# Two-layer routed FFN around causal linear attention: the third norm's moments in two halves, and the state's copy and mask moved to ScalarE and GpSimd

## The reference

```
def _layernorm(x, axis=-1, eps=1e-05):
    return (x - mean) / sqrt(var + eps)

def _L0_ffn_ref(x, Wg, W1, b1, W2, b2):            # 8 experts, 128 -> 512 -> 128
    top_w, top_i = top_k(x @ Wg, 2); top_w = softmax(top_w)
    for i in range(8):
        out_i = gelu(x @ W1[i] + b1[i]) @ W2[i] + b2[i]
        results = results + w_per_expert[..., i:i+1] * out_i

def _L0_attn_ref(x, ...):                          # 16 heads of 8
    q, k = phi(x @ Wq.T + bq), phi(x @ Wk.T + bk)  # phi = elu + 1
    v = x @ Wv.T + bv
    kv_prefix = cumsum(k outer v, axis=tokens);  k_prefix = cumsum(k)
    out = (q . kv_prefix) / (q . k_prefix + 1e-6)
    return merge_heads(out) @ Wo.T + bo

x = x + 0.5 * ffn(layernorm(x))
x = x + attn(layernorm(x))
x = x + 0.5 * ffn(layernorm(x))
```

## Time and profile before

| | |
|---|---|
| median of 3 runs | 378.76 us (378.44 to 379.9) |
| profiled execution, its own time | 379.24 us |
| its span, first to last instruction | 377.5 us |
| busy: PE / DVE / POOL / ACT | 81% / 61% / 60% / 33% |
| attention loop (164.4 to 238.4 us), busy: PE / DVE / POOL / ACT | 65.66 / 68.57 / 42.84 / 31.62 us |
| ScalarE's waits for stores of the ring | 6.7 us in 6 |

### The profile page before, as it was taken

How to read it: one execution, slowest core, us unless ns; L and a number is a source line. 1 busy time by engine, 2 the same in 40 slices (tenths; PEclk the granted TensorE clock), 3 DMA queues, 4 the chain that set the end, 5 groups by cost and what they waited for, 6 DMA issues and landing times.

```text
span 377.5 us, 7941 instructions
## 1 busy us (share of the span) xinstructions
PE 305.7 (81%) x1941; PEld 241.6 (64%) x1942; DVE 229.1 (61%) x620; ACT 122.8 (33%) x344; POOL 226.0 (60%) x266
## 2 busy tenths in 40 slices
PE   2984799898989975689999997557989888989950
PEld 1932499787878861256767675423989777878820
DVE  6899344334333337979989898995344433433456
ACT  2206243322323340234444553253333232332300
POOL 5037577777777770264584845265577777777720
PEclk9997699999999997589999999665899999999995
DMA  7530466555545527100000000013565555545347
GB/s 214 166 102 2 113 191 183 151 159 163 150 144 166 142 71 202 29 0 0 3 0 10 14 16 16 21 43 106 125 193 161 160 160 142 168 137 156 112 130 224
DMA packets 34918, 41.90 MB, mean 111 GB/s; under 512 B 4753, under 2 KB 21265, under 8 KB 34898
## 3 DMA queue, kind: packets, MB, share of 16 engines
q1 hardware_dynamic: 29906, 31.44, 30.0%
q0 software_dynamic: 4992, 10.23, 8.9%
HBM read 33.39 MB, written 8.26 MB: 110 GB/s over the span
## 4 chain that ended last, share of the span: by engine, by line
POOL 33%; PE 26%; DVE 13%; DMA 12%; issue 12%; ACT 2%; SPq 0%; POOLq 0%; DVEq 0%; ACTq 0%
POOL y_rows L405 15%; POOL xg L398 13%; PE banks L987 5%; PE banks L1093 5%; DMA xg<-xn_rows,src_row 4%; PE banks L996 3%; DMA y_rows<-y_tile,dst_row 3%; DMA xn_rows<-xn_ring 2%; POOL kv L427 2%; DMA y_back<-y_rows 2%; DVE x L789 2%; PE banks L1072 2%; PE banks L917 2%; DVE x L794 2%; DVE beats L651 1%
## 5 line engine op out<-in xcount | busy, mean ns | idle before, releaser
L398 POOL DMA_INDIRECT xg<-xn_rows,src_row x78 | 75.5, 968 | 33.3 <-issue 23.4
L405 POOL DMA_INDIRECT y_rows<-y_tile,dst_row x78 | 76.8, 985 | 24.6 <-issue 21.4
L987 PE MATMUL banks<-xgT,w1b 128*128 128x128 f32 x624 | 88.3, 286 | 0.8 <-ACT xgT L507 0.8
L996 PE MATMUL banks<-w,h_act 128*128 x624 | 87.7, 284 | 0.4 <-issue 0.2
L746 DVE TENSOR_TENSOR h_pre<-banks,w1b 128x512 f32<-128x512 f32 x78 | 53.9, 691 | 55.6 <-PE banks L987 51.5
L987 PEld LDWEIGHTS banks<-xgT,w1b 128*128 128x128 f32 x624 | 78.3, 197 | 2.7 <-issue 1.2
L996 PEld LDWEIGHTS banks<-w,h_act 128*128 128x128 f32 x624 | 75.5, 191 | 5.8 <-issue 2.6
L756 DVE COPY y_tile<-banks 128x128 f32<-128x128 f32 x78 | 22.7, 292 | 65.5 <-DMA y_rows<-y_tile,dst_row 57.9
L507 ACT COPY xgT<-banks 128x128 f32<-128x128 f32 x78 | 20.7, 265 | 126.1 <-PE banks L1006 126.1
L514 ACT ACTIVATE h_act<-h_pre 128x512 f32<-128x512 f32 x78 | 49.3, 632 | 4.7 <-DVE h_pre L746 4.7
L427 POOL TENSOR_TENSOR kv<-qk,vx 128x1024 f32<-128x1024 f32 x16 | 31.5, 1970 | 29.8 <-DVE qk L775 29.8
(11 more groups left out here) (185 smaller groups left out, 395.3 us busy)
## 6 DMA issues: line engine op xcount, KB each, us to landing
w1b<-in_W1b SPq DMA_DIRECT2D x78, 258.0 KB
y_back<-y_rows SPq DMA_DIRECT2D x16, 256.0 KB, 4.9
xg<-xn_rows,src_row POOLq DMA_INDIRECT x78
y_rows<-y_tile,dst_row POOLq DMA_INDIRECT x78
x<-in_L_attn_x SPq DMA_DIRECT2D x4, 256.0 KB, 3.6
xn_rows<-xn SPq DMA_DIRECT2D x4, 256.0 KB, 3.0
xn_rows<-xn_ring SPq DMA_DIRECT2D x16, 64.0 KB, 1.5
out<-x SPq DMA_DIRECT2D x4, 256.0 KB, 2.9
```

Of the source, the lines that this page charges most:

```text
L398: g.indirect_dma_start(out=xg[:, n % RING, :], out_offset=None, in_=xn_rows[f][:, :], in_offset=bass.IndirectOffsetOnAxis(ap=src_row[:, n: ...
L405: g.indirect_dma_start(out=y_rows[f][:, :], out_offset=bass.IndirectOffsetOnAxis(ap=dst_row[:, i:i + 1], axis=0), in_=y_tile[:, i % RING, ...
L987: last = mm(h_bank(q)[:, c * P:(c + 1) * P], w1b[:, q, c * P:(c + 1) * P], xgT[:, q, :], start=True, stop=True)
L996: last = mm(y_bank(r), h_act[:, r, c * P:(c + 1) * P], w2[:, bass.ds(col + c * P, P)], start=(c == 0), stop=(c == FC - 1))
```

## The change

The third norm's work on GpSimd is cut in two: the seven instructions come behind `outer` of tiles 7, 11 and 15, and 1/root and shift in a function of their own, `ln3_roots`, behind `outer` of tiles 9 and 13 and behind the loop. VectorE's L859 is gone: ScalarE copies the state out of PSUM to a new tile `state_raw`, behind `pre` and in front of the next `norm`, and GpSimd multiplies that by the mask (`own_heads`), for tile i-1 at the end of its work for tile i. The state matmul of the last tile is left out. `norm_3` writes to `xn`, which the first FFN no longer needs, and no ring is left; its lag is 11 tiles for 8, and SyncE stores four tiles at a time.

```
                 else:
-                    rows = xn_rows[1].rearrange("(t p) d -> t p d", p=P)
-                    for t in range(NT):
-                        sp.wait_ge(xn_ready, NT + t + 1)
-                        sp.wait_ge(xn_stored, 16 * (NC + t))
-                        sp.dma_start(rows[t], xn_ring[:, t % 2, :]).then_inc(xn_stored, 16)
+                    rows = xn_rows[1].rearrange("(t p) d -> p t d", p=P)
+                    for c in range(NC):
+                        sp.wait_ge(xn_ready, NT + CH * (c + 1))
+                        sp.dma_start(rows[:, c * CH:(c + 1) * CH, :], xn[:, c * CH:(c + 1) * CH, :]).then_inc(xn_stored, 16)
...
-                pool.wait_ge(xn_stored, 16 * (NC + NT * f))
+                pool.wait_ge(xn_stored, 16 * NC * (f + 1))
...
                 g.tensor_tensor(var_3[:, :], var_3[:, :], apart_3[:, :], ALU.add).then_inc(ln3_step, 1)
+
+            def ln3_roots(b):
+
+                t = b * CH
                 pool.wait_ge(ln3_step, b * 7 + 7)
                 g.tensor_tensor(rstd_3[:, t:t + CH], var_3[:, :], minus_half[:, 0:CH], ALU.pow).then_inc(ln3_root, 1)
...
+            def own_heads(i):
+
+                pool.wait_ge(raw_sb, i + 1)
+                pool.wait_ge(inter_ps, i + 1)
+                g.tensor_tensor(state[:, :], state_raw[:, :], head_mask[:, :, :].rearrange("p e h -> p (e h)"),
+                                ALU.mult).then_inc(state_sb, 1)
 
             for i in range(NT):
                 outer(i)
...
-                if i >= CH + 2 and i % CH == 2:
+                if i > CH and i % CH == 3:
                     ln3_moments(i // CH - 1)
+                if i > 2 * CH and i % CH == 1:
+                    ln3_roots(i // CH - 2)
+                if 0 < i:
+                    own_heads(i - 1)
+            ln3_roots(NC - 2)
             ln3_moments(NC - 1)
+            ln3_roots(NC - 1)
             ffn_moves(1)
...
             def norm_3(t):
 
                 act.wait_ge(ln3_ready, t // CH + 1)
-                if t >= 2:
-                    act.wait_ge(xn_stored, 16 * (NC + t - 1))
-                s.activation(xn_ring[:, t % 2, :], x[:, t, :], ACT.Identity,
+                s.activation(xn[:, t, :], x[:, t, :], ACT.Identity,
...
-            NORM_LAG = 2 * CH
+            NORM_LAG = 2 * CH + 3
...
                     turned_3(i - 2, xn_bank)
+                if i + 1 < NT:
+                    act.wait_ge(state_ps, i + 1)
+                    at_least(act, state_sb, i)
+                    s.copy(state_raw[:, :], state_bank).then_inc(raw_sb, 1)
                 if i + 3 < NT:
                     norm(i + 3)
...
                 v.tensor_scalar(den[:, :], nd[:, DH, :], ATT_EPS, None, ALU.add).then_inc(den_sb, 1)
-                dve.wait_ge(state_ps, i + 1)
-                v.tensor_tensor(state[:, :], state_bank, head_mask[:, :, :].rearrange("p e h -> p (e h)"),
-                                ALU.mult).then_inc(state_sb, 1)
                 dve.wait_ge(den_sb, i + 1)
...
-                mm(state_bank, qk[:, r, P:2 * P], vx[:, r, :, :].rearrange("p e h -> p (e h)"),
-                   start=(i == 0), stop=True, skip_group_check=True).then_inc(state_ps, 1)
+                if i + 1 < NT:
+                    mm(state_bank, qk[:, r, P:2 * P], vx[:, r, :, :].rearrange("p e h -> p (e h)"),
+                       start=(i == 0), stop=True, skip_group_check=True).then_inc(state_ps, 1)
```

More of the change, by code:

```diff
@@ L172, in macaron_kernel @@
         y_back = sb("y_back", [P, TOPK, NT, P])
-        xn_ring = sb("xn_ring", [P, 2, P])
         xa = sb("xa", [P, 2, P])
@@ L184, in macaron_kernel @@
         state = sb("state", [P, H * VE])
+        state_raw = sb("state_raw", [P, H * VE])
         prod = sb("prod", [P, VE * P])
@@ L228, in macaron_kernel @@
         qT_ps, qT_sb, kv_sb, prefix_ps = map(sem, ("qT_ps", "qT_sb", "kv_sb", "prefix_ps"))
-        state_ps, state_sb = map(sem, ("state_ps", "state_sb"))
+        state_ps, state_sb, raw_sb = map(sem, ("state_ps", "state_sb", "raw_sb"))
         prod_sb, local_sb, nd_sb, den_sb, rden_sb = map(sem, ("prod_sb", "local_sb", "nd_sb", "den_sb", "rden_sb"))
```

## The result

| | before | changed |
|---|---|---|
| median | 379.04 us (378.44 to 379.9, 4 runs) | 375.64 us (375.37 to 376.1, 4 runs) |
| ratio | | 0.9888 (95% interval 0.9848 to 0.9929) |
| profiled execution, its span | 379.24, 377.5 us | 376.1, 374.0 us |
| prod(2) to prod(15) in attention | 60.09 us | 58.02 us |
| lane numbers to the read of the sum, second routing | 9.60 us | 8.83 us |

The account below looks back on a forecast made before the run. GpSimd bounds the expert stages; in attention VectorE and the path through kv are both nearly tight. 3.0 + 0.8 + 0.8 = 4.6 us off gave a forecast of 374.4 us, 8-in-10 range 373.0 to 376.4, own range 373.6 to 375.4.

Parts of the forecast that it names:

- Moments split: Attention loop, GpSimd: splitting the third norm's work leaves no kv late and removes three stalls of 1.01 us, 3.0 us.
- Routing's end: Second routing, lane numbers to read of the sum: ScalarE on time saves 0.8 us; GpSimd's last hot vector is late next.
- Norm_3, stores: Behind attention: later norm_3 without ring and four larger stores end in time; neither is on the path, so no cost.
- Masking on GpSimd and copy on ScalarE: Attention loop: masking takes 0.49 us, copy 0.28; masked state at E+1.6 or E+2.05 (E: kv's end), with 0.8 us slack.
- Rival 3: Attention loop: masking ahead of kv in GpSimd's queue makes each of 14 kv 0.5 us late; 381.2 us, chance 0.05.
- VectorE without the mask: Attention loop: removing VectorE's mask instruction is worth 0.09 us a tile, not its 0.30 duration; 0.8 us in all.
- rival 2: Attention loop: GpSimd's masking collides with VectorE's merged and holds it, losing 1.3 to 3.3 us; 375.7 to 377.7, chance 0.14.
- The row I held against the rule: Attention loop: merged kept 0.37 us beside a 0.20 us GpSimd instruction, so no row shows the skill's wait for short ones.
- The loop of two tiles: Attention: 4.77 us through kv plus VectorE's 4.01 make 8.78 us per two tiles, 4.39 a tile.
- 0.11 x 13 + 0.4: Attention loop: upper bound for VectorE without the mask, stated as 1.9 us; the lower bound was 0.

Follow-up runs that it names:

- experiment 1: Kernel before with only norm_3's ring removed, lag 11 for 8 and four stores of four tiles: 420.51 us against 420.01 before, ratio 0.9985.
- experiment 6: Changed kernel with den computed from PSUM plus local and issued ahead of nd: median 411.25 us, ratio 0.9842 to before; loop 56.30 us.
- Experiments 1 to 4: Kernel before with ring and lag alone, 420.51 us; changed with mask on VectorE, 416.13; before with mask's move alone, 423.02; changed with copy later, 416.68.
- experiment 3: Kernel before with only the state's copy and mask moved, last state matmul dropped, moments whole, ring kept: median 423.02 us, ratio 1.0077.

## Why the prediction was right, and where it was not

*Moments split, 3.0 us:* right. Alone it gave 3.01 us against a profile in which TensorE's clock never fell at a late kv; where it does fall (experiment 1), the split is worth more. Seven instructions, masking and next kv fit: in GpSimd's tile 7 (VectorE's tile 6) the masking ended at 196.94 and kv started at 197.52, at phi + 0.49.

*Routing's end, 0.8 us:* right, 0.77 us, with GpSimd the last as named. *Norm_3, stores:* right at zero.

*Masking on GpSimd and copy on ScalarE:* the sizes were right (0.49 and 0.28 us; masked state 1.5 to 1.7 us behind kv's end in common tiles, 1.9 behind seven instructions), and no kv and no reader waited. Rival 3, every kv late, did not come: in the changed kernel kv starts 0.49 to 0.50 us behind phi in all tiles from 2 on.

*VectorE without the mask, 0.8 us:* the step that failed. The reading of the rows held where nothing collides: rden 0.20 us behind den, prod to phi 3.91 us, and prod(1) to prod(2) at 4.26. But I priced a place on GpSimd by its own engine's time alone. The loop's part of the term came out as 60.09 - 58.02 - 3.01 = -0.9 us where +0.6 was forecast. The ends gave 0.1 us each, as forecast, so the whole term is -0.75 where +0.8 stood. The sum 3.01 - 0.75 + 0.77 is 3.0 us, as the rows have it (phi(0) to the read of the sum: 99.03 us before, 96.00 changed). The forecast as such, the likeliest case, was therefore wrong, and rival 2 was what happened: 1.5 us lost to the masking beside a VectorE instruction, in its stated 1.3 to 3.3. It had the mechanism and one victim: merged's rows grew by 0.3 us in all, in three tiles, where 0.35 us each was stated. The larger victim, den, whose rows grew by 1.5 us in five tiles, was not named, so that the loss falls in rival 2's span is partly chance. It could have been named: by the prediction's own rows den stands in the masking's way. It starts at E+1.18 (209.25 - 208.07), and the masking was placed at E+1.07 to E+1.56. The cited section of the Trainium skill covers it too, as a tensor_scalar from SBUF to SBUF; the prediction drew on its other half alone. The row I held against the rule, a GpSimd instruction of 0.20 us beside merged, was no witness: it ended 0.10 us into merged, and a whole masking that ends 0.13 us into merged leaves it at 0.37 us too (experiment 6, tile 4).

*The loop of two tiles,* 4.77 us through kv plus VectorE's own part: right, and tested beyond the change: with prod to phi at 3.81 it gives 4.29 a tile, and experiment 6 alternates 4.43 and 4.16.

*The rest.* That the range held is in part its width: it took in rival 2's milder half. A slip in a bound changes nothing: 0.11 x 13 + 0.4 is 1.8 us, not 1.9. By the rows the change gives 3.0 us, by the spans 3.5, so half a microsecond of the result is luck. In the changed kernel's profile phi(0) came 0.6 us later than before, in a part that was not changed, and the last expert stage took 101.17 us for 102.35. Experiments 1 to 4 ran the first expert stage, the same in all of them, in 120.9 to 122.9 us on one chip, so a microsecond either way there is not the change's.

## What to carry to other kernels

Moving an instruction from VectorE to GpSimd is priced at the places where it will run beside VectorE: list VectorE's instructions around it that read two SBUF tensors or go from SBUF to SBUF with a scalar, and give those another operand or another place before you move anything (den here got both, PSUM and a place ahead of the masking). What a removed instruction is worth is the distance between starts that really closes (0.09 us of 0.30), and only as far as the other loop through the same buffers lets it.

## What the runs showed of the hardware that was not expected

- A held VectorE instruction shows as a longer one, with no idle time in front of it: den up to 0.56 us for 0.16, ending 0.03 to 0.04 us behind GpSimd's instruction, merged up to 0.71 for 0.37, ending 0.24 to 0.25 behind the masking in every tile where it is held. In the waits it appears nowhere.
- So an overlap at merged's start is free: it keeps 0.37 to 0.38 us when the masking ends up to 0.13 us into it (experiment 6, tiles 4, 7, 9 and 11).
- den can be held by a GpSimd instruction whose row starts 0.03 us after its own (205.89 and 205.92), and is not held by one that starts 0.05 us after it (200.54 and 200.59).
- A wait of TensorE for GpSimd sometimes took its granted clock down and sometimes not: 1.68 us did in experiment 1 (0.57 over the next four microseconds), 1.67 us at the same place in the kernel before did not; in experiment 3, one kernel, 1.49 us did and 1.47 us did not. In experiment 1 the stall of 1.0 us became 2.6.
- Expert stages of the same program took 101 to 103 us on one chip and 119 to 124 us on others, with the attention loop the same to 0.1 us.
